# Three of pair 1's weight folds at the end of the first layer instead of at the opening of attention

## What is computed

```python
def _L1_xattn_ref(hidden_q, kv_c, Wq, w_kc_q, w_kc_kv, W_qr, W_kr, Wo):
    q_hk = (hidden_q @ Wq.T).reshape(Bv, Sv, H, K)
    q_big = jnp.einsum('bshk,hkq->bshq', q_hk, w_kc_q)
    q_big = _apply_rope(q_big, sin_q[None, :, None, :], cos_q[None, :, None, :])
    kv_r = _apply_rope(kv_c, sin_k[None], cos_k[None])
    q_r = jnp.einsum('bshq,hqr->bhsr', q_big, W_qr)
    k_r = jnp.einsum('bld,hdr->bhlr', kv_r, W_kr)
    scores = jnp.einsum('bhsr,bhlr->bhsl', q_r, k_r)
    attn = jax.nn.softmax(scores, axis=-1)
    ctx_c = jnp.einsum('bhsl,bld->bhsd', attn, kv_r)
    ctx_lat = jnp.einsum('bhsd,hkd->bhsk', ctx_c, w_kc_kv)
    ctx = ctx_lat.transpose(0, 2, 1, 3).reshape(Bv, Sv, H * K)
    return ctx @ Wo.T
...
    x = x + jnp.tanh(g_ffn[0]) * _L0_ffn_ref(_layernorm(x, axis=-1), L0_ffn_Wr, L0_ffn_br, L0_ffn_W1, L0_ffn_W2)
    x = x + jnp.tanh(g_xattn[1]) * _L1_xattn_ref(_layernorm(x, axis=-1), ctx_512, L1_xattn_Wq, ...)
```

## Time and profile before

| | us |
|---|---|
| runs of the kernel before | 474.36, 474.98, 478.52 |
| median | 474.98 |
| profiled execution | 475.87 |
| its span | 474.0 |
| its mean granted TensorE clock, as a share of full speed | 0.971 |

### The profile page before, as it was taken

One profiled execution on the slowest core, in us unless ns is written; L12 is line 12 of the kernel. 1 busy time (PEld: TensorE's weight loads), 2 busy tenths in 40 slices (PEclk: granted clock), 3 DMA queues, 4 the chain that ended last, 5 costly groups with the idle time before them and its releaser, 6 DMA issues. The chain is left out here.

```text
span 474.0 us, 8851 instructions
## 1 busy us (share of the span) xinstructions
PE 438.7 (93%) x2723; PEld 279.3 (59%) x2723; DVE 304.0 (64%) x886; ACT 252.0 (53%) x628; POOL 188.0 (40%) x190
## 2 busy tenths in 40 slices
PE   5886999899969999999999999999998899899987
PEld 2574877786734555555555555555566773644476
DVE  3989799955145766677676667757743748446612
ACT  3582445545314677667767766776666242045510
POOL 1650404041603566555465655546643005543000
PEclk9995999999977999999999999999999979999999
DMA  7643000000102343343334334212200799589202
GB/s 249 190 110 103 3 0 1 1 2 22 46 0 66 90 102 90 77 115 74 94 80 105 89 75 107 50 44 57 66 12 2 204 309 278 143 188 261 72 29 90
DMA packets 61448, 43.81 MB, mean 92 GB/s; under 512 B 22955, under 2 KB 54502, under 8 KB 61414
## 3 DMA queue, kind: packets, MB, share of 16 engines
q1 hardware_dynamic: 60646, 41.04, 32.6%
q0 software_dynamic: 768, 2.36, 2.5%
HBM read 27.25 MB, written 2.23 MB: 62 GB/s over the span
## 5 line engine op out<-in xcount | busy, mean ns | idle before, releaser
L1172 POOL TENSOR_TENSOR PB<-PB,inv 128x512 f32<-128x512 f32 x64 | 66.6, 1041 | 79.6 <-DVE inv L1222 79.4
L1111 ACT ACTIVATE PB<-ps,low 128x256 f32<-128x256 f32 x128 | 59.6, 471 | 31.0 <-DVE low L1216 31.0
L275 POOL TENSOR_TENSOR rot<-rot 128x512 f32<-128x512 f32 x48 | 61.1, 1273 | 32.6 <-DMA rot<-rot 32.6
L1216 DVE TENSOR_REDUCE low<-ps 128x2 f32<-128x512 f32 x64 | 44.1, 689 | 38.4 <-PE ps L1028 37.4
L255 DVE TENSOR_TENSOR rot<-ps,sinq 128x512 f32<-128x512 f32 x48 | 33.2, 692 | 16.6 <-PE ps L242 14.5
L1036 PE MATMUL ps<-ident,PB 128*128 128x128 f32 x256 | 41.1, 283 | 1.1 <-ACT PTS L1119 0.8
L1119 ACT ACTIVATE PTS<-ps 128x512 f32<-128x512 f32 x64 | 38.2, 597 | 7.2 <-PE ps L1036 5.1
L1036 PEld LDWEIGHTS ps<-ident,PB 128*128 128x128 f32 x256 | 27.7, 141 | 24.0 <-issue 19.9
L242 PE MATMUL ps<-XH,CH 128*128 128x512 f16 x96 | 37.6, 392 | 0.0
L242 PE MATMUL ps<-XL,CH 128*128 128x512 f16 x96 | 37.4, 390 | 0.0
L242 PE MATMUL ps<-XH,CL 128*128 128x512 f16 x96 | 37.4, 390 | 0.0
(11 more groups left out here) (246 smaller groups left out, 874.0 us busy)
## 6 DMA issues: line engine op xcount, KB each, us to landing
rot<-rot SPq DMA_DIRECT2D x64, 128.0 KB, 2.3
rot<-rot SPq DMA_DIRECT2D x64, 64.0 KB, 2.0
EGU<-in_L_ffn_W_gate_dram SPq DMA_DIRECT2D x8, 384.0 KB, 5.7
EGU<-in_L_ffn_W_up_dram SPq DMA_DIRECT2D x8, 384.0 KB, 5.8
ED<-in_L_ffn_W_down_dram SPq DMA_DIRECT2D x8, 384.0 KB, 6.6
rot<-in_L_ffn_W_dram SPq DMA_DIRECT2D x2, 1024.0 KB, 10.1
WQ<-in_L_xattn_Wq_dram SPq DMA_DIRECT2D x8, 256.0 KB, 3.0
WO<-in_L_xattn_Wo_dram SPq DMA_DIRECT2D x8, 256.0 KB, 3.1
```

The source lines that it names most:

```text
L275: pool.tensor_tensor(g.RO[:, n, x, :], g.RO[:, n, x, :], g.TC[x][:, :], ALU.add).then_inc(g.sum_ok, 1)
L1111: e = act.activation(PB[t % 2][:, h, :], g.ps[:, SC + t % 2, h * S:(h + 1) * S], ACT.Exp, bias=low[:, t % 2, h:h + 1], scale=-1.0, accum_o ...
L1172: pool.tensor_tensor(PB[t % 2][:, :, :], PB[t % 2][:, :, :], inv[:, t % 2, :].unsqueeze(2).broadcast_to([P, 2, S]), ALU.mult).then_inc(nor ...
L1216: dve.tensor_reduce(low[:, t % 2, :], g.ps[:, SC + t % 2, :].rearrange("p (h s) -> p h s", h=2), AX.X, ALU.min).then_inc(low_ok, 1)
```

## The change

Folds 0, 1 and 2 of pair 1 leave the attention block's opening and go to the end of the first layer's block: fold 0 ahead of the context product, fold 1 between it and the last norm's transpositions, fold 2 behind these. They use PSUM banks 1, 0 and 3. As in the rest of that block, ScalarE writes a full copy besides the high part for folds 0 and 1, and GpSimd makes the low part. In ScalarE's list fold 0 stands ahead of the norm's square root, fold 1 between the context copies and XH, fold 2 at the end. The opening of attention keeps folds 3, 4 and 5, each followed by a query product (3, 4, 5). The semaphores' starting values follow.

```diff
--- before.py
+++ after.py
@@ -228,6 +228,7 @@
 
 
 GROUPS_Q = 2 * QT
+EARLY_FOLDS = 3
 QA, QP = 0, 2
 HI = [slice(0, DC), slice(DC, P)]
 SWAPS = (2 * 16, 2 * 16, 4 * 16)
@@ -382,7 +383,7 @@
         splits = lambda n: sum(is_split[0:n + 1])
         plain = lambda n: n + 1 - splits(n)
 
-        fold_bank = lambda k: g.ps[:, (N_FOLD + k) % 4, :]
+        fold_bank = lambda k: g.ps[:, QA if k == FOLDS + 1 else (N_FOLD + k) % 4, :]
 
         def wait_empty(eng, n):
 
@@ -495,6 +496,8 @@
                         masked(b, n)
                         if b == B - 1 and n >= 1:
                             add_partners(pool, g, 0, n - 1)
+                for k in range(FOLDS, FOLDS + 2):
+                    fold_second(k)
 
             @block.tensor
             def _(pe):
@@ -682,9 +685,20 @@
                         second_norm(b - 1)
                 result(B - 1, UNITS - 2)
                 result(B - 1, UNITS - 1)
+
+                def next_fold(f):
+
+                    fold_product(pe, g, 1, f, fold_bank(FOLDS + f)).then_inc(filled, 1)
+
+                pe.wait_ge(g.d_w[1], DW)
                 pe.wait_ge(gelu_ok, UNITS * B)
+                next_fold(0)
                 context_product(pe, g, 0, 0, 0)
+                pe.wait_ge(g.rope_ok, QT + ROPE0)
+                next_fold(1)
                 second_norm(B - 1)
+                pe.wait_ge(ms_ok, UNITS * B)
+                next_fold(2)
 
             @block.scalar
             def _(act):
@@ -782,9 +796,12 @@
                             mask(b, n)
                         if b >= 1 and n == (2 if b == B - 1 else UNITS - 1):
                             second_norm(b - 1)
+                fold(FOLDS)
                 norm_root(act, g, n2, B - 1)
                 context_keep(act, g, 0, 0, 0)
+                fold(FOLDS + 1)
                 second_norm(B - 1)
+                fold(FOLDS + 2)
 
             @block.vector
             def _(dve):
@@ -962,7 +979,7 @@
 
         EXP0, TPS0, TOK0, CXPS0, CXOK0, FOLD0 = 2, 2, 1, 2, 1, 1
 
-        DONE, NSPLIT = FOLDS, len(FOLD_SPLIT)
+        DONE, NSPLIT = FOLDS + EARLY_FOLDS, len(FOLD_SPLIT) + sum(f in FOLD_SPLIT for f in range(EARLY_FOLDS))
         starts = [(exp_ok, EXP0), (t_ps, TPS0), (t_ok, TOK0), (cx_ps, CXPS0), (cx_ok, CXOK0),
                   (fold_ok, DONE + FOLD0), (fold_ps, DONE), (fold_hi, NSPLIT)]
 
@@ -1087,10 +1104,9 @@
                         turn(p, 0)
 
                 pe.wait_ge(credit, 1)
-                for f in range(FOLDS):
+                for f in range(EARLY_FOLDS, FOLDS):
                     fold(1, 1, f)
-                    if f < QT:
-                        queries(0, 0, QT + f)
+                    queries(0, 0, QT + f - EARLY_FOLDS)
                 pairs(pe, step, cross)
                 turn(PAIRS - 1, LAST)
                 attend(PAIRS - 1, B - 1)
@@ -1249,10 +1265,9 @@
                         attended(p - 1, B - 1)
 
                 dve.wait_ge(credit, 1)
-                for f in range(FOLDS):
+                for f in range(EARLY_FOLDS, FOLDS):
                     fold(1, 1, f)
-                    if f < QT:
-                        rotate(0, QT + f)
+                    rotate(0, QT + f - EARLY_FOLDS)
                 pairs(dve, step, cross)
                 attended(PAIRS - 1, B - 2)
                 attended(PAIRS - 1, B - 1)
```

## The result

The changed kernel is slower: 479.65 us median of 22 executions (474.9 to 481.85), against 475.06 of the kernel before (22, 473.95 to 478.92); ratio 1.0073, 95% interval 1.005 to 1.0097. Its executions lie in two groups, ten between 474.9 and 478.1 and twelve between 479.5 and 481.9. The profiled one took 480.88 with a span of 479.1, so it belongs to the upper group.

The account below looks back on a forecast made before the run. TensorE alone was taken to bound the kernel from 155.25 on; `turn(0, 0)` 0.75 to 1.35 us earlier, less 1.4 given back to the clock, made 0.05 to 0.65 slower, forecast as 474.8 us, no change, range 472.4 to 477.2.

Parts of the forecast that it names:

- The bound from 155.25 on: From `turn(0, 0)` to the end of attention TensorE alone sets the pace, at clock 1.00.
- The opening at full clock: Opening of attention: three folds and three query products alternating take 5.99 us at full clock.
- The late block end: First layer's end: ScalarE's later copies delay the opening by 0.9 us, bounds 0.5 and 1.5.
- What is late next: After the opening: GpSimd's in-order additions hold `turn(0, 0)` until 7.3 us after the last query product.
- The hole: Ahead of `turn(0, 0)`: TensorE stands idle for 3.8 us in one piece.
- three signs of being wrong: Around `turn(0, 0)` and the block's end: hole missing, clock after it staying 1.00, or block's end not later.
- the sum's clock terms: Lower clock in the opening, leaving 0.75 to 1.35 us gain, and behind the hole, giving back 1.4.
- with the lower clock until 143.6, as now: Opening: 4.7 us at the lower clock do 2.35 us of work, so scores start at 147.2.
- E = 147.2: Last query product's end, equal to the scores' start; `turn(0, 0)` then at 154.5, 0.75 us earlier.
- 1.0 to 1.7, I take 1.4: Behind the hole ahead of `turn(0, 0)`: us lost to the lower clock on the TensorE-bound stretch.
- the gain of 3.05 us in my best case: Opening at full clock: scores start at 144.9 and `turn(0, 0)` comes at 152.2, 3.05 us earlier.
- (2): Hole ahead of `turn(0, 0)` brings 7 us of lower clock; 1.5 to 2.5 us slower, 476.5 to 477.5; chance 0.2.

Follow-up runs that it names:

- a_fill: Changed kernel with 14 unused matmuls on TensorE in the hole ahead of `turn(0, 0)`; 475.36 us, 0.9992 of the kernel before.
- a_port_table: Changed kernel with an unused square root ahead of fold 0's copies and GpSimd's first subtraction held until XN; 474.81 us, 1.0028 of the kernel before.
- a_fill_end: Changed kernel with eight unused matmuls at the first block's end, hole left as it is; 475.5 us, 1.0013 of the kernel before.
- b_pool_first: Kernel before with GpSimd's normalisation of tile 0 ahead of its third addition; 475.06 us, 1.0009 of the kernel before.
- a_one_fold: Changed kernel with only fold 0 moved to the first layer's end, five folds in the opening; 475.59 us, 0.9996 of the kernel before.
- a_pool_first: Changed kernel with GpSimd's normalisation of tile 0 ahead of its third addition; 472.5 us, 0.9896 of the kernel before.
- a_both_table: Changed kernel, queries 4, 5 before folds 4, 5, tile 0's normalisation before GpSimd's third addition, early unused square root; 470.57 us, 0.9915 of the kernel before.

## Why the prediction was wrong

**What held.** The bound from 155.25 on: `turn(0, 0)` to the third block is 213.90 in six of the profiles, those in which TensorE never stood idle for more than 1.6 us in front of it and GpSimd's order was the old one. The opening at full clock: 5.99 predicted, 6.02 measured in four profiles. The late block end in size only: 0.9 predicted, 0.71 measured, and that they are close is partly luck. I had the context copies late behind fold 0, which is right for 0.44 of the 0.71 us, but then went over fold 1's copies, XH and XL, where the path is the context copies, VectorE's context rest of 1.39 us and XL; and the load of the square root's table, in ScalarE's idle time before (127.68 to 128.96), I had not seen at all. What is late next: 7.3 us from the last query product to `turn(0, 0)`, measured 157.17 - 149.94 = 7.23, with the two normalisations behind the third addition. The hole: 3.8 predicted, 3.60 measured. None of the three signs of being wrong that I named (no hole, full clock behind it, no later block end) occurred.

**What failed is the sum's clock terms, twice.** Both were sizes; their places were right. First, "with the lower clock until 143.6, as now" was my worst case for the opening, E = 147.2. In the profile the opening ran at clock 0.55 nearly to its end, 10.27 us, and E was 149.94. My own durations held the bound: 1.65 us for a fold at half clock against 0.82, so the whole opening at half clock is up to twice 5.99. I took for a bound what one execution had shown. Instead of 0.75 us earlier, `turn(0, 0)` came 1.92 later on the profile's own scale, 0.94 later counted from the residual. Second, "1.0 to 1.7, I take 1.4" for the clock behind the hole. It was 2.5 us, and 2.5 to 2.8 (216.41, 216.45 and 216.71) in the three profiles with a hole over 3.5 us and nothing in it, because all 5.13 us behind `turn(0, 0)` ran at the lower level; I had read the price from the shorter of the two low stretches of the trace. The two mistakes have one sign, and together `turn(0, 0)` and the stretch behind it are 0.94 + 2.51 = 3.45 us late. A third point was left out: I measured every gain against an opening of before that had 5.6 us at the lower clock. At full clock on both sides the change is worth nothing (20.35 us against 20.66 and 20.73), so even the gain of 3.05 us in my best case was clock.

**The rival that came true.** It is (2), slower by the hole's clock, to which I gave 0.2; its place and mechanism are shown by a_fill. Its price of 1.5 to 2.5 was too small, since beside the hole it counted on a gain ahead of it; the median was 4.6 us higher, the mean 3.1 to 3.4. The range ended at 477.2, inside the lower group of executions, and twelve of the 22 lie at 479.5 or above. The question that would have led there is how much time the lower clock could take if both idle stretches, the block's end and the hole, hit in one execution. I treated them as alternatives, each with a chance. They are two events in one execution. The profiles fit this: with the hole and a slow opening the changed kernel took 480.88, in the upper group, and with the hole and a full-clock opening a_port_table took 474.21 and a_fill_end 475.65, in the lower. No profile of an execution of the changed kernel's own lower group was taken.

The Trainium skill ("TensorE: Matmul & The Clock Gate", section "HAM oscillation — how this bites in real kernels") had named the mechanism, that a long wait in a matmul stream is paid again behind it; a_fill agrees, 213.90 us behind the filled hole against 216.41 behind the empty one. The Trainium skill ("SBUF — State Buffer", section "SBUF: two separate sides") says that a VectorE operation in a two-port mode, or one with two inputs in SBUF beside a GpSimd operation that reads SBUF, takes a port pair that GpSimd shares, as an exclusive lock: the one that starts first holds it, the other waits. The variance fits it: it ended at 134.36 + 0.69 = 135.05, right behind GpSimd's subtraction (134.11 + 0.91 = 135.02), and took 0.17 us with GpSimd held back; in which mode it ran no row shows.

**What stays open.** Why the changed opening stayed at the lower clock for nearly all of it, where the one before recovered on the way. From mean clock and length, the low part of a slow opening was 5.6 to 6.0 us in before, b_pool_first and a_one_fold, 9.2 in the changed kernel and a_pool_first, and 2.8 in a_both_table; no experiment exchanged the folds alone. Open too is what, beside the filled hole, made a_fill's mean 3.3 us lower, and whether fold 0 behind the context product would give back the 0.46 us of the block's end.

## What to carry to other kernels

When work leaves a stretch on the critical engine, follow the in-order queue of each helper engine from the last input that stays where it was: here the last query product stayed sixth of six, and GpSimd's queue turned the gain into a hole. Work that doesn't feed the chain (folds 4 and 5) belongs behind the product that does, and the consumer that is ready first (the normalisation) ahead of the one that still waits for a DMA. An idle gap on TensorE has to be priced with the clock behind it, and over several executions: read the mean granted clock of each before trusting one trace.

## What the runs showed that I had not expected

Fourteen useless matmuls in a wait made the changed kernel 3.3 us faster in the mean, 2.5 of it shown behind the hole, and thirteen in the idle time at a block's end make the kernel before 0.3% faster. A hole of 3.6 to 3.8 us cost 2.5 to 2.8 us behind it in each of the three profiles that have it, while holes of 1.57 and 1.58 us cost nothing (213.90). One kernel can have two groups of times, 4.3 us apart in their means (476.7 and 481.0), that differ in the time at the lower clock, 22 to 28 us against 29 to 35. And a VectorE operation on 128x2 elements took 0.69 us for 0.17 while a GpSimd subtraction ran.
